# Moving loads, stores and vector work of a fused attention and dense kernel to other places and queues

## The chip, the cores and the metric

The kernel runs on one core of a Trainium2 chip. The metric is the device time in microseconds (us). An engine is one of PE (TensorE), DVE (VectorE), ACT (ScalarE), POOL (GpSimd) and SP (SyncE, which here only issues DMAs). The engines run their own instruction streams and meet at semaphores.

## The reference

The computation is cross attention followed by a 4-bit quantised dense layer, each with a layernorm ahead and a residual around it. All of it is float32.

```python
x = x + xattn(layernorm(x), ctx, ctx, pos, mask, Wq, Wk, Wv, Wo)   # x, ctx: (8, 256, 1024)
# xattn: 32 query heads, 8 key/value heads of 128; rope on q and k; masked softmax; @ Wo
x = x + (layernorm(x) @ W + bias)      # W = scales * (nibbles(qweight) - nibbles(qzeros))
```

## The kernel before

Every float32 product is made of three PE passes: each operand is split into a high part (a rounded copy, made by ACT) and a low part (the rest, a subtraction on DVE or POOL), and `products` multiplies high by high, high by low and low by high. So all operands pass through ACT and then through DVE or POOL before PE can use them.

The order of work is written out by hand, one stream per engine, in three stages:

1. **Keys and values.** 64 units of 24 matmuls each; the results go to scratch in DRAM. During the first key units DVE takes the statistics of the rows of x. `inverse_std` turns them into 1/std, PE transposes mean and 1/std in the value units `V_H0_N1` (L625 to L631), DVE copies them out (L1223 to L1227), and SP stores them and goes on with its queue (L358).
2. **Attention.** 16 groups (G) of 8 units (u8), one unit for each of 4 batches and 2 head pairs. In a unit PE computes scores of the next unit (12 short matmuls), half a query tile (12 matmuls), the weighted values of the unit two back (6 matmuls) and the other half of the query tile (12). The probabilities are transposed in a round trip: DVE writes `squares`, SP stores them (`store_squares`, L424), waits until they have landed, loads them back turned (`load_turned`, L434), ACT and POOL split them (L969, L1548), PE weighs. SP's stream is in order, so all its other loads and stores stand between these. Group 7 is the **switch**: the normalised activations `act_t` of the first half of the batches are replaced with those of the second, in eight pieces of 512 KB. Pieces 0 to 3 are for token half c=0 and 4 to 7 for c=1. Each piece is loaded into the low half (`load_next`, by SP), copied by ACT (`split_next`, L885) and subtracted by DVE (`rest_of_next`, L1175); PE waits for pairs of them (`next_lo`, L723, L730) in units 4 and 6. Also here DVE writes the masks of the second half (`set_mask`, L1256), and the rope tables are loaded.
3. **Output product and dense layer.** The product with Wo is done as seven half-size products M1 to M7 of 16 steps each (112 steps, counted s). A step needs a left tile (`xring`, from `left_scratch`) and one or two right blocks (`wraw`), loaded two steps ahead by `load_step(s)`, which waits until both operands of step s-2 are split. POOL adds the right blocks (`right_summed`, L1578), ACT splits, POOL and DVE take the low parts (`step_lo`), PE does 24 matmuls. Within the first ten steps the last attention results (pairs q = 62 and 63) are still combined (`combine`, POOL, five additions) and stored (`store_outputs`, `store_sums`, SP). From step 26 to 49 DVE and ACT unpack the dense weights between steps, and at each product's end (s = 17, 33, 49, ...) DVE adds eight PSUM banks into `rows` (`product_out`), which PE must await bank by bank before it starts the next product.

Of the kernel before, what the change touches and what calls it, by code (L numbers as in the profile page):

```python
# [9 lines left out]
F32 = mybir.dt.float32  # L10
# [59 lines left out]
def build(nc, x, ctx_t, x_tiles, x_pieces, pos, mask, wq, wk, wv, wo, qweight, qzeros, scales, bias, table, ident, out):  # L70
# [4 lines left out]
    with ExitStack() as stack:  # L75
# [208 lines left out]
        def _(sp):  # L284
# [97 lines left out]
            for u in range(16):  # L382
                g = u // 2
                if u % 2 == 0:
                    i = KVH + g + 2
# [62 lines left out]

            def load_next(i):

                sp.wait_ge(xc_stored[i % 4], 32)
                sp.wait_ge(q_done, 62 + 2 * (i // 4))
                sp.dma_start(next_rows(i, 1).bitcast(F32), xc_dram[i]).then_inc(next_in[i], 16)

            def attention(G, half, first=False, last=False, switch=False):
                g, nh = (0, 1) if switch else (G - half * 8 + 1, half)
                for u8 in range(UPG):
# [34 lines left out]
                    if switch:  # L492
                        if 2 <= u8 <= 5:
                            load_next(2 * u8 - 4)
                            load_next(2 * u8 - 3)
                        if u8 in (3, 5):
                            c = (u8 - 3) // 2
                            sp.wait_ge(q_rot, 62 + 2 * c)
                            sp.dma_start(rope[:, c, :, :], rope_dram[1, c]).then_inc(rope_in[c], 16)
# [43 lines left out]
            for s in range(4, STEPS):  # L543
                load_step(s)

                if s in (5, 7):
                    q = 62 + (s - 5) // 2
                    store_outputs(q, 31, q % 2)
                if s in (6, 9):
                    q = 62 + (s - 6) // 3  # L550
                    store_sums(q, 31, q % 2)
                if s < 20:
                    r = (s - 4 + 8) % 16
                    sp.dma_start(rows[:, r, :], x_rows[row_tile(r)]).then_inc(rows_in[r // 8], 16)

                if s == 20:
                    sp.dma_start(packed, qweight).then_inc(dense_in, 16)
                if s == 21:
                    sp.dma_start(scale_rows, scales.rearrange("r (a n) -> r a n", a=1).broadcast_to([KT, P // KT, E])
                                 ).then_inc(dense_in, 16)  # L560
                if s == 22:
                    sp.dma_start(zero_words[:, :],
                                 qzeros.rearrange("g (a w) -> g a w", a=1).broadcast_to([KT, P // KT, E // NIB])
                                 ).then_inc(dense_in, 16)
                if s == 23:
                    sp.dma_start(bias_rows[:, :], bias.rearrange("(a n) -> a n", a=1).broadcast_to([P, E])
                                 ).then_inc(bias_in, 16)
# [7 lines left out]
        def _(pe):  # L575
# [49 lines left out]
            for t in range(TT):  # L625
                value_unit(V_H0_N1 + t, items=C_WV1 if t == 0 else None)
                if t == 2:

# [196 lines left out]
        def _(act):  # L825
# [52 lines left out]
            def tile_hi(t):  # L878
                act.wait_ge(x_centred, 8 + t + 1)
                act.wait_ge(kv_done, V_H1_N0 + t + 1)  # L880
                act.activation(act_v[:, 0, :, t * P:(t + 1) * P], x_tile[t % 4], ACT.Copy).then_inc(x_hi, 1)

            def split_next(i):
                act.wait_ge(next_in[i], 16)
# [108 lines left out]
            def attention(G, first=False, last=False, switch=False):  # L993
                for u8 in range(UPG):
# [7 lines left out]
                    if switch and 3 <= u8 <= 6:  # L1002
                        split_next(2 * u8 - 6)
                        split_next(2 * u8 - 5)
                    if not (last and u8 >= 5):
                        i = (u8 + 3) % 4

                        scored = G * 16 + (2 * (u8 + 1 - i) + (0 if i < 2 else 4))
                        query_hi(TILES[i], G * UPG + (u8 + 3), None if first and u8 == 0 else scored)
                    if u8 < UPG - 1:  # L1010
                        nxt, nG = u8 + 1, G
# [18 lines left out]
                    if not (last and u8 == UPG - 1):  # L1030
                        scaled(nG, nxt)


# [26 lines left out]
            for s in range(2, STEPS):  # L1060
                step_hi(s)
                if s >= 28 and s % 3 == 1 and s < 52:
                    dense_hi((s - 28) // 3)
                if s == 92:
# [21 lines left out]
        def _(dve):  # L1086
# [134 lines left out]
            for t in range(TT):  # L1221
                value_lo(V_H0_N1 + t)
                if t == 3:  # L1223
                    dve.wait_ge(moments_turned, 1)
# [90 lines left out]
            def attention(G, half, first=False, switch=False, last=False):  # L1315
                for u8 in range(UPG):
# [33 lines left out]
                    if not (last and u8 == UPG - 1):  # L1350
                        inverse_sum(nG, nxt)
                    if switch and u8 >= 6:

                        for b1 in range(2):
                            set_mask(2 * (u8 - 6) + b1, 1)
                    if last and u8 in (6, 7):
# [64 lines left out]
            for s in range(2, STEPS):  # L1421
# [7 lines left out]
                step_lo(s)  # L1429
                if s == 26:  # L1430
                    dve.wait_ge(dense_in, 48)
                    for i in range(NIB):
                        dve.tensor_scalar(zeros_f.rearrange("p (w i) -> p w i", i=NIB)[:, :, i], zero_words[:, :],
                                          BITS * i, 2 ** BITS - 1, ALU.logical_shift_right,
                                          ALU.bitwise_and).then_inc(z_step, 1)
                if s == 27:
                    dve.wait_ge(z_step, NIB)
                if 27 <= s < 51:
                    if s % 3 == 0:
                        dense_full((s - 27) // 3)  # L1440
                    if s % 3 == 1:
                        dense_lo((s - 28) // 3)
                if 82 <= s < 90:
# [35 lines left out]
        def _(pool):  # L1479
# [134 lines left out]
            for s in range(2, STEPS):  # L1614
                step_lo(s)
                if s + 1 < STEPS:
                    right_summed(s + 1)
                if s in (3, 4, 6, 7):
                    q = 62 + (s - 3) // 3
                    combine(q, q % 2, s % 3)  # L1620
            pool.wait_ge(bias_in, 16)
# [38 lines left out]
```

## Time and profile before

| | |
|---|---|
| median of 3 runs | 2292.0 us (2291.43 to 2292.24) |
| the profiled execution, its device time | 2291.43 us |
| its span from first to last instruction | 2289.6 us |
| PE / DVE / ACT / POOL busy | 98% / 59% / 45% / 60% |
| DMA | 208 GB/s over the span |
| clock of PE granted over the span | 0.994 |

Span and device time differ by 1.8 us. PE's busy time leaves 55 us of the span. The trace has further stretches in which PE is busy but at the lower of its two clocks (granted 0.5 of full speed); a window's granted clock below 1.00 shows these.

### The profile page before, as it was taken

The numbers are of one execution on the slowest core, as the hardware profiler recorded it, in microseconds if no ns is written. First come the engines' busy times: TensorE is split into PE (matmuls) and PEld (weight loads), VectorE is DVE, ScalarE is ACT, GpSimd is POOL, SyncE is SP. The second block draws the span as 40 slices with busy tenths as digits, with TensorE's granted clock in tenths as the row PEclk, the third lists the DMA queues.
The fourth block names the chain that finished last, engine by engine and source line by source line (L and its number), as shares of the span: only waits on it lengthen the run. The fifth ranks groups of instructions, "written<-read, shape, count | busy, mean of one in ns | idle before, by whom it ended". The sixth has DMA issues, their size and how long they took to land.

```text
span 2289.6 us, 33278 instructions
## 1 busy us (share of the span) xinstructions
PE 2234.6 (98%) x10562; PEld 1865.2 (81%) x10562; DVE 1350.1 (59%) x2535; ACT 1040.8 (45%) x2264; POOL 1382.3 (60%) x981
## 2 busy tenths in 40 slices
PE   8999999999999998899999999899999999999999
PEld 6888887888888887688888888678887787878887
DVE  4772574777777777777777777423775324433432
ACT  3222123766776766667666676523332232321000
POOL 1320544788888986788888888665663353454210
PEclk9999999999999999999999999999999999999999
DMA  7766674678778878787878778587563454452111
GB/s 260 258 238 218 242 260 150 213 238 258 239 247 246 251 242 259 221 247 243 247 244 257 240 245 262 165 310 265 186 198 128 151 194 154 148 183 84 47 47 46
DMA packets 300779, 476.71 MB, mean 208 GB/s; under 512 B 23552, under 2 KB 195872, under 8 KB 300704
## 3 DMA queue, kind: packets, MB, share of 16 engines
q1 hardware_dynamic: 286624, 440.12, 59.8%
q10 hardware_dynamic: 13312, 33.56, 3.7%
q0 software_dynamic: 768, 2.10, 0.3%
q8 instruction: 39, 0.64, 0.1%
q14 instruction: 36, 0.29, 0.0%
HBM read 303.70 MB, written 171.98 MB: 208 GB/s over the span
## 4 chain that ended last, share of the span: by engine, by line
PE 84%; DVE 4%; DMA 4%; POOL 3%; SPq 2%; issue 1%; ACT 1%; ACTq 0%; POOLq 0%; DVEq 0%
PE ps L236 20%; PE ps L237 20%; PE ps L238 20%; PE ps L775 8%; PE ps L777 8%; PE ps L776 8%; DMA sq_scratch<-scores 3%; DVE rows L1392 1%; SPq L434 1%; PE ps L799 1%; DMA act_t<-xc_scratch 1%; POOL rope_tmp L1488 1%; POOL s_buf L1488 0%; DVE a_parts L1282 0%; DVE rows L1394 0%
## 5 line engine op out<-in xcount | busy, mean ns | idle before, releaser
L236 PE MATMUL ps<-act_t,wq_t 128*128 128x512 f32 x1280 | 502.2, 392 | 15.7 <-DVE act_t L1175 9.3
L237 PE MATMUL ps<-act_t,wq_t 128*128 128x512 f32 x1280 | 501.1, 392 | 0.0
L238 PE MATMUL ps<-act_t,wq_t 128*128 128x512 f32 x1280 | 499.4, 390 | 0.0
L1566 POOL TENSOR_TENSOR b_parts<-wraw,b_parts 128x512 fp32r<-128x512 f32 x112 | 196.5, 1754 | 277.2 <-ACT b_parts L991 277.2
L775 PE MATMUL ps<-b_parts,a_parts 128*128 128x512 f32 x896 | 352.3, 393 | 9.2 <-DVE rows L1392 4.9
L1282 DVE TENSOR_TENSOR a_parts<-xring,a_parts 128x1024 fp32r<-128x1024 f32 x112 | 147.5, 1317 | 344.4 <-ACT a_parts L986 344.4
L777 PE MATMUL ps<-b_parts,a_parts 128*128 128x512 f32 x896 | 349.5, 390 | 0.0
L776 PE MATMUL ps<-b_parts,a_parts 128*128 128x512 f32 x896 | 349.2, 390 | 0.0
L1548 POOL TENSOR_TENSOR q_t<-pt_raw,q_t 128x1024 fp32r<-128x1024 f32 x124 | 298.8, 2410 | 80.0 <-ACT q_t L969 78.3
L986 ACT ACTIVATE a_parts<-xring 128x1024 fp32r<-128x1024 f32 x112 | 118.8, 1060 | 421.7 <-PE ps L777 417.2
L236 PEld LDWEIGHTS ps<-act_t,wq_t 128*128 128x128 f32 x1280 | 241.8, 189 | 64.7 <-DVE act_t L1175 10.3
L1488 POOL TENSOR_TENSOR rope_tmp<-rope_tmp 128x512 f32<-128x512 f32 x144 | 193.5, 1344 | 155.1 <-DVE rope_tmp L1114 154.4
L238 PEld LDWEIGHTS ps<-act_t,wq_t 128*128 128x128 f32 x1280 | 241.3, 189 | 51.4
L237 PEld LDWEIGHTS ps<-act_t,wq_t 128*128 128x128 f32 x1280 | 241.8, 189 | 45.4
L951 ACT ACTIVATE probs<-scores,neg_max 128x256 f32<-128x256 f32 x512 | 253.9, 497 | 9.8 <-DVE neg_max L1271 9.6
L1112 DVE TENSOR_TENSOR rope_tmp<-ps,rope 128x512 f32<-128x512 f32 x144 | 99.4, 690 | 211.2 <-PE ps L238 190.3
L961 ACT ACTIVATE probs<-probs,inv_sum 128x256 f32<-128x256 f32 x512 | 216.9, 495 | 1.8 <-DVE inv_sum L1278 1.8
L943 ACT ACTIVATE q_t<-rope_tmp 128x512 fp32r<-128x512 f32 x128 | 81.0, 633 | 294.4 <-POOL rope_tmp L1488 294.4
L775 PEld LDWEIGHTS ps<-b_parts,a_parts 128*128 128x128 f32 x896 | 168.5, 188 | 55.8 <-DVE rows L1392 8.7
L1537 POOL TENSOR_TENSOR q_t<-rope_tmp,q_t 128x512 fp32r<-128x512 f32 x128 | 196.1, 1532 | 20.3 <-ACT q_t L943 20.2
L777 PEld LDWEIGHTS ps<-b_parts,a_parts 128*128 128x128 f32 x896 | 168.5, 188 | 35.3
L776 PEld LDWEIGHTS ps<-b_parts,a_parts 128*128 128x128 f32 x896 | 168.6, 188 | 33.8
(129 smaller groups left out, 4329.1 us busy)
## 6 DMA issues: line engine op xcount, KB each, us to landing
sq_scratch<-scores SPq DMA_DIRECT2D x124, 512.0 KB, 4.7
pt_raw<-sq_scratch SPq DMA_DIRECT2D x496, 128.0 KB, 3.1
xring<-left_scratch SPq DMA_DIRECT2D x112, 512.0 KB, 3.9
left_scratch<-s_buf SPq DMA_DIRECT2D x64, 640.0 KB, 4.8
wraw<-in_L_xattn_Wq SPq DMA_DIRECT2D x64, 512.0 KB, 4.8
wraw<-in_L_xattn_Wo SPq DMA_DIRECT2D x64, 512.0 KB, 4.8
v_scratch<-kv_t ACTq DMA_DIRECT2D x32, 512.0 KB, 3.2
k_scratch<-kv_t ACTq DMA_DIRECT2D x32, 512.0 KB, 4.9
```

What stands on the lines that cost most here:

```text
L236: eng.matmul(dst, lh, rh, start=(k == first), stop=False)
L237: eng.matmul(dst, lh, rl, start=False, stop=False)
L238: mm = eng.matmul(dst, ll, rh, start=False, stop=(k == last))
L775: pe.matmul(dst, lh, rh, start=(begins and not onto), stop=False, skip_group_check=True)
L776: pe.matmul(dst, lh, rl, start=False, stop=False, skip_group_check=True)
L777: mm = pe.matmul(dst, ll, rh, start=False, stop=ends, skip_group_check=True)
L951: e = act.activation(probs[:, par, j, qt, :], score_v[:, par, j, qt * S:(qt + 1) * S], ACT.Exp, bias=neg_max[:, par, j, qt:qt + 1], scale= ...
L961: e = act.activation(probs[:, par, j, qt, :], probs[:, par, j, qt, :], ACT.Copy, scale=inv_sum[:, par, j, qt:qt + 1])
L1488: pool.tensor_tensor(tmp[:, 0, :], tmp[:, 0, :], tmp[:, 1, :], ALU.add).then_inc(done, 1)
L1537: pool.tensor_tensor(q_parts[:, c, j, 1, :], rope_tmp[:, 0, :], q_parts[:, c, j, 0, :].bitcast(F32), ALU.subtract).then_inc(q_lo, 1)
L1548: pool.tensor_tensor(lo, pt_raw[:, u8 % 2, :], hi.bitcast(F32), ALU.subtract).then_inc(pt_lo, 1)
L1566: pool.tensor_tensor(b_parts[:, s % 2, 1, :], wraw[s % 2][:, 0:NW], b_parts[:, s % 2, 0, :].bitcast(F32), ALU.subtract).then_inc(right_lo, 1)
```

## The change

The change has five parts.

- **Activation pieces at the switch.** `load_next` leaves SP's stream. ACT issues the pieces, four at once, after `query_hi` in units 2 and 4. ACT's `split_next` calls are spread: one before `query_hi` and one at the end of a unit, from the end of unit 2 to unit 6.
- **Masks at the switch.** One `set_mask` at the end of each of units 3 to 6 instead of two at the end of units 6 and 7.
- **Moments.** The two PE transposes and DVE's copy stand one value unit earlier.
- **Last results.** POOL combines q = 62 wholly after step 3 and q = 63 after step 5. SP stores both the outputs and the sums of each ahead of `load_step(5)` and `load_step(7)`.
- **Dense weights.** The four loads are issued together at s = 20 (before, at 20 to 23), and unpacking runs from s = 23 to 46 (before, 26 to 49).

```diff
-            def load_next(i):
-                sp.wait_ge(xc_stored[i % 4], 32)
-                sp.wait_ge(q_done, 62 + 2 * (i // 4))
-                sp.dma_start(next_rows(i, 1).bitcast(F32), xc_dram[i]).then_inc(next_in[i], 16)
...
-                        if 2 <= u8 <= 5:
-                            load_next(2 * u8 - 4)
-                            load_next(2 * u8 - 3)
...
             for s in range(4, STEPS):
-                load_step(s)
-
                 if s in (5, 7):
                     q = 62 + (s - 5) // 2
                     store_outputs(q, 31, q % 2)
-                if s in (6, 9):
-                    q = 62 + (s - 6) // 3
                     store_sums(q, 31, q % 2)
+                load_step(s)
...
-                if t == 2:
+                if t == 1:
                     pe.wait_ge(ln_ready, 1)
...
+            def load_next(c):
+                for b in range(4):
+                    act.wait_ge(xc_stored[b], 32)
+                act.wait_ge(q_done, 62 + 2 * c)
+                for i in range(4 * c, 4 * c + 4):
+                    act.dma_start(next_rows(i, 1).bitcast(F32), xc_dram[i]).then_inc(next_in[i], 16)
...
                     if switch and 3 <= u8 <= 6:
-                        split_next(2 * u8 - 6)
                         split_next(2 * u8 - 5)
...
+                    if switch and u8 in (2, 4):
+                        load_next(u8 // 2 - 1)
...
+                    if switch and 2 <= u8 <= 5:
+                        split_next(2 * u8 - 4)
...
-                    if switch and u8 >= 6:
-                        for b1 in range(2):
-                            set_mask(2 * (u8 - 6) + b1, 1)
+                    if switch and u8 >= 3 and u8 < 7:
+                        set_mask(u8 - 3, 1)
...
-                if 27 <= s < 51:
+                if 24 <= s < 48:
                     if s % 3 == 0:
-                        dense_full((s - 27) // 3)
+                        dense_full((s - 24) // 3)
...
-                if s in (3, 4, 6, 7):
-                    q = 62 + (s - 3) // 3
-                    combine(q, q % 2, s % 3)
+                if s in (3, 5):
+                    q = 62 + (s - 3) // 2
+                    for part in range(2):
+                        combine(q, q % 2, part)
```

ACT's stream in the switch, from `query_hi` of unit 2 on, before:

```order
L943 ACTIVATE q_t<-rope_tmp 128x512
L951 ACTIVATE probs,row_sum<-scores,neg_max 128x256 x4
L969 ACTIVATE q_t<-pt_raw 128x1024
L961 ACTIVATE probs<-probs,inv_sum 128x256 x4
L843 ACTIVATE wq_t<-wraw 128x8x128
L885 ACTIVATE act_t<-act_t 128x2x512 x2
L943 ACTIVATE q_t<-rope_tmp 128x512
```

and the same place of the change, where `act_t<-xc_scratch` are the pieces' loads and `act_t<-act_t` their copies:

```order
L936 ACTIVATE q_t<-rope_tmp 128x512
L874 DMA act_t<-xc_scratch 128x2x512 x4
L944 ACTIVATE probs,row_sum<-scores,neg_max 128x256 x4
L962 ACTIVATE q_t<-pt_raw 128x1024
L954 ACTIVATE probs<-probs,inv_sum 128x256 x4
L878 ACTIVATE act_t<-act_t 128x2x512
L828 ACTIVATE wq_t<-wraw 128x8x128
L878 ACTIVATE act_t<-act_t 128x2x512
L936 ACTIVATE q_t<-rope_tmp 128x512
```

Four loads now stand ahead of the exponentials of unit 2, and one copy has moved ahead of the head split (`wq_t<-wraw`).

SP's queue from the loads of step 5 to those of step 7, before (`left_scratch<-o_buf` are outputs, `left_scratch<-s_buf` are sums):

```order
L515 DMA xring<-left_scratch 128x2x512
L521 DMA wraw<-in_L_xattn_Wo 128x512
L522 DMA wraw<-in_L_xattn_Wo 128x512
L441 DMA left_scratch<-o_buf 128x256
L442 DMA left_scratch<-o_buf 128x256
L554 DMA rows<-in_x 128x1024
L515 DMA xring<-left_scratch 128x2x512
L521 DMA wraw<-in_L_xattn_Wo 128x512
L522 DMA wraw<-in_L_xattn_Wo 128x512
L447 DMA left_scratch<-s_buf 128x5x256
L554 DMA rows<-in_x 128x1024
L515 DMA xring<-left_scratch 128x2x512
```

and in the change, from after the rows of step 4 to the first load of step 6:

```order
L441 DMA left_scratch<-o_buf 128x256
L442 DMA left_scratch<-o_buf 128x256
L447 DMA left_scratch<-s_buf 128x5x256
L506 DMA xring<-left_scratch 128x2x512
L512 DMA wraw<-in_L_xattn_Wo 128x512
L513 DMA wraw<-in_L_xattn_Wo 128x512
L543 DMA rows<-in_x 128x1024
L506 DMA xring<-left_scratch 128x2x512
```

The loads of step 5 now stand behind the sums of q = 62, which wait for POOL.

DVE's stream at the end of product M4, s = 48 and 49, before:

```order
L1282 TENSOR_TENSOR a_parts<-xring,a_parts 128x1024 x2
L1399 TENSOR_SCALAR dense<-dense 128x1024
L1402 TENSOR_TENSOR dense<-dense 128x1024
L1404 TENSOR_TENSOR dense<-dense 128x1024
L1392 TENSOR_TENSOR rows<-ps,rows 128x512 x16
L1282 TENSOR_TENSOR a_parts<-xring,a_parts 128x1024
```

and in the change:

```order
L1403 TENSOR_TENSOR w_parts<-dense,w_parts 128x1024
L1278 TENSOR_TENSOR a_parts<-xring,a_parts 128x1024 x2
L1387 TENSOR_TENSOR rows<-ps,rows 128x512 x16
L1278 TENSOR_TENSOR a_parts<-xring,a_parts 128x1024 x16
```

No unpacking stands between the last left tile and the 16 additions any more.

## Rows read from the trace of the kernel before

**Rows 1.** PE's waits: who, for whom, us in total, times, longest.

```profile
PE ps L236 <- DVE act_t L1175: 9.3, 2, 8.5
...
PE ps L236 <- DVE wq_t L1103: 0.6, 2, 0.4
```

**Rows 2.** Windows: stretch, length, each engine's busy us, granted clock, DMA share, GB/s.

```profile
840.00:860.00 20.00, 20.00 (x105) 17.19 (x104) 15.17 (x34) 15.70 (x38) 17.44 (x13) 1.00 0.80 256
880.00:900.00 20.00, 13.47 (x54) 10.67 (x53) 13.88 (x26) 11.50 (x23) 12.37 (x10) 0.83 0.94 298
...
1720.00:1740.00 20.00, 17.32 (x67) 12.77 (x66) 15.72 (x19) 5.69 (x7) 5.44 (x4) 0.91 0.35 119
1740.00:1760.00 20.00, 19.36 (x83) 15.04 (x83) 7.92 (x9) 4.83 (x7) 5.47 (x3) 1.00 0.40 130
...
1820.00:1840.00 20.00, 18.94 (x79) 14.02 (x78) 13.45 (x20) 5.56 (x7) 8.30 (x6) 1.00 0.58 193
```

**Rows 3.** Timeline of DVE in the switch: start, us, line, operation, idle before.

```profile
875.72 0.69 DVE L1112 TENSOR_TENSOR rope_tmp<-ps,rope 128x512 f32<-128x512 f32 x1 [1.84 <-PE ps L238]
887.53 1.23 DVE L1175 TENSOR_TENSOR act_t<-act_t 128x1024 fp32r<-128x1024 f32 x1 [0.66 <-ACT act_t L885]
937.52 4.07 DVE L1256 TENSOR_SCALAR scores<-mask 128x512 f32<-128x512 uint8 x2
957.25 0.69 DVE L1112 TENSOR_TENSOR rope_tmp<-ps,rope 128x512 f32<-128x512 f32 x1 [1.94 <-PE ps L238]
```

**Rows 4.** Timeline of PE in the switch, matmuls after long waits.

```profile
891.07 0.77 PE L236 MATMUL ps<-act_t,wq_t 128*128 128x512 f32 x1 [5.69 <-issue]
925.99 0.79 PE L236 MATMUL ps<-act_t,wq_t 128*128 128x512 f32 x1 [8.50 <-DVE act_t L1175]
```

**Rows 5.** Chain of waits in the switch: start, us, what.

```profile
872.61 4.80 DMA sq_scratch<-scores
...
905.38 9.34 DMA sq_scratch<-scores
```

**Rows 6.** Timeline of SP and ACT around unit 2 of the switch.

```profile
879.53 1.19 SPq L453 DMA_DIRECT2D act_t<-xc_scratch  x2
870.96 0.63 ACT L943 ACTIVATE q_t<-rope_tmp 128x512 fp32r<-128x512 f32 x1 [2.31 <-POOL rope_tmp L1488]
875.45 1.06 ACT L969 ACTIVATE q_t<-pt_raw 128x1024 fp32r<-128x1024 f32 x1 [1.77 <-DMA pt_raw<-sq_scratch]
```

**Rows 7.** Timeline of PE and DVE around the transposed moments.

```profile
159.33 0.27 PE L630 MATMUL ps<-identity,mean_var 128*16 128x128 f32 x1
157.61 0.17 DVE L1160 TENSOR_TENSOR inv_std<-ln_tmp 128x16 f32<-128x16 f32 x1
```

**Rows 8.** Timeline of SP in steps 5 and 7 of the output product.

```profile
1482.46 0.38 SPq L515 DMA_DIRECT2D xring<-left_scratch  x1
1492.95 0.39 SPq L447 DMA_DIRECT2D left_scratch<-s_buf  x1
```

**Rows 9.** Timeline of POOL and ACT in the same steps.

```profile
1484.83 0.74 POOL L1557 TENSOR_TENSOR s_buf<-o_buf 128x256 f32<-128x256 f32 x1
1492.81 1.29 POOL L1566 TENSOR_TENSOR b_parts<-wraw,b_parts 128x512 fp32r<-128x512 f32 x1
1501.91 2.23 POOL L1578 TENSOR_TENSOR wraw<-wraw 128x512 f32<-128x512 f32 x1 [3.21 <-DMA wraw<-in_L_xattn_Wo]
1489.79 1.06 ACT L986 ACTIVATE a_parts<-xring 128x1024 fp32r<-128x1024 f32 x1 [3.86 <-PE ps L777]
...
1530.11 1.07 ACT L986 ACTIVATE a_parts<-xring 128x1024 fp32r<-128x1024 f32 x1 [4.00 <-PE ps L777]
```

**Rows 10.** Timeline of DVE and PE at the end of product M4.

```profile
1728.19 1.78 DVE L1399 TENSOR_SCALAR dense<-dense 128x1024 int32<-128x1024 int32 x1
1732.41 9.65 DVE L1392 TENSOR_TENSOR rows<-ps,rows 128x512 f32<-128x512 f32 x16
1733.84 0.47 PE L775 MATMUL ps<-b_parts,a_parts 128*128 128x512 f32 x1 [2.48 <-DVE rows L1392]
```

More of the change, by code:

```diff
@@ L557, in _ @@
                     sp.dma_start(packed, qweight).then_inc(dense_in, 16)
-                if s == 21:
                     sp.dma_start(scale_rows, scales.rearrange("r (a n) -> r a n", a=1).broadcast_to([KT, P // KT, E])
                                  ).then_inc(dense_in, 16)
-                if s == 22:
                     sp.dma_start(zero_words[:, :],
@@ L564, in _ @@
                                  ).then_inc(dense_in, 16)
-                if s == 23:
                     sp.dma_start(bias_rows[:, :], bias.rearrange("(a n) -> a n", a=1).broadcast_to([P, E])
@@ L1061, in _ @@
                 step_hi(s)
-                if s >= 28 and s % 3 == 1 and s < 52:
-                    dense_hi((s - 28) // 3)
+                if s >= 25 and s % 3 == 1 and s < 49:
+                    dense_hi((s - 25) // 3)
                 if s == 92:
@@ L1222, in _ @@
                 value_lo(V_H0_N1 + t)
-                if t == 3:
+                if t == 2:
                     dve.wait_ge(moments_turned, 1)
@@ L1429, in _ @@
                 step_lo(s)
-                if s == 26:
+                if s == 23:
                     dve.wait_ge(dense_in, 48)
@@ L1435, in _ @@
                                           ALU.bitwise_and).then_inc(z_step, 1)
-                if s == 27:
+                if s == 24:
                     dve.wait_ge(z_step, NIB)
-                if 27 <= s < 51:
+                if 24 <= s < 48:
                     if s % 3 == 0:
-                        dense_full((s - 27) // 3)
+                        dense_full((s - 24) // 3)
                     if s % 3 == 1:
-                        dense_lo((s - 28) // 3)
+                        dense_lo((s - 25) // 3)
                 if 82 <= s < 90:
```

## The prediction

> **What bounds the kernel now.** I read the page first: PE is busy for 98% of the span, so a change pays only where PE waits or where it delays PE. Next came PE's waits. The longest single one, 8.5 us, is for DVE L1175, the low parts of the pieces at the switch [rows 1]. The windows then show where time is lost. Around the switch PE has 13.47 us of work in 20 and a granted clock of 0.83, while 20 us at 840 are full. At 1720, the end of M4, it has 17.32 us at 0.91, and 19.36 in the next 20 [rows 2]. A clock of 0.91 over 20 us is some 3.6 us at the lower level (1.2 GHz instead of 2.4), which costs half of that, 1.8 us. It follows an idle of 2.48 us [rows 10]. In the switch, idles of 5.69 and 8.50 us precede or meet the lower clock [rows 4]. I take it that each idle as long as these costs another 1.7 to 1.8 us.
>
> What the switch costs comes from DVE's rotations, one per unit. From 875.72 to 957.25 there are seven intervals, 81.53 us [rows 3]. A full unit is 8.26 us: 30 long matmuls, one per 0.227, make 6.8, and twelve short ones at 0.12 make 1.4 (PE works without a gap there, the window at 840 [rows 2]). Seven are 57.8. So the switch costs 23.7 us.
>
> **Part 1, the switch.** Now the pieces are issued at 879.53, behind SP's wait for the squares stored at 872.61 [rows 5, 6]. The data is free earlier: `query_hi` of unit 2 (870.96) already implies that PE is done with token half c=0. After the change four issues of 0.59 us (half of 1.19 for two) begin there, so the exponentials start 1.8 us later, at 873.4, and end at 875.4. ACT waited 1.77 us for the turned probabilities until 875.45 anyway, so this costs nothing. I follow the chain with the durations of the trace:
>
> - ACT rescales by 878.3, copies piece 0 (1.06), splits the head and copies piece 1 by 881.3.
> - DVE, done with the row maxima at 880.9, subtracts pieces 0 and 1 (1.23 each [rows 3]) by 883.3 and the head by 884.6. PE wants them at 885.4, after the scores of unit 4. The wait of 5.69 us goes.
> - Pieces 2 and 3: ACT copies the latter by 889.9. DVE rotates (2.1), transposes (1.25) and subtracts both by 891.8. The mask that now ends unit 3 falls beside POOL's 2.4 us subtraction. The masks of 937.52 took 4.07 us for two beside POOL's work [rows 3], so it may add up to 2: 893.8. PE wants them at 889.5. New wait: 2.3 to 4.3.
> - Pieces 4 and 5 are issued at 890 and copied by 899.6, subtracted by 903.0, wanted at 904.1: no wait. Piece 7 is subtracted at 910.4, wanted at 908.3: a wait of 2.1, where 8.50 stood.
>
> That is 4.4 to 6.4 us. But the DMA engines must carry it. Normal units use them at 0.80 with 256 GB/s, the switch at 0.94 with 298 [rows 2], so about 317 GB/s is full. The eight pieces and two rope tables are 5.2 MB, 14 to 16 us of full DMA; in the 42 us from 871 to 913 some 8.5 are free. The lack of 6 to 8 us is not on top of the waits, since they give it time, but the larger counts: 8. With one more stretch at the lower clock (1.7 to 1.8) the switch costs 10 instead of 23.7: **-13.7**. Bounds: the chain alone with no clock loss costs 5 (-18.7); a store of squares as slow as the one of 905.38, 9.34 us instead of 4.80 [rows 5], in each of the units costs 17 (-6.7). The masks no longer delay the first unit of group 8; this is inside.
>
> The Trainium skill (DMA: Bandwidth & Descriptors, section on queues, rings and completion order) says that each DMA engine takes turns between the queues that have work. By that rule SP's squares get only a part of the engines while ACT's 2 MB are in the queue, and the sum would lean to the upper bound, -6.7. The trace does not show the two queues together in this stage.
>
> **Part 2, the moments.** The transposes run at 159.33 [rows 7], right behind the third value unit. That unit is 24 matmuls at 0.227, so the second ends at 153.9, and the transposes now stand there. They need 1/std, which DVE finishes at 157.78; nothing of that chain waits for PE. At their old place that was 1.5 us in time. PE will idle 3.9 us. All work up to the attention hangs on PE's units, and from there to 384 PE has only two waits, 0.6 us in all, for DVE L1103 [rows 1], so nothing gives it back. An idle of 3.9 should bring the lower clock once: **+5.6** (3.9 + 1.7). Bounds: 3.3 if the later small idles close up, 7.3 with two such stretches. The earlier copy of the moments helps transfers that PE did not wait for: nothing.
>
> **Part 3, the last results.** In M1 PE needs 24 matmuls at 0.227, 5.44 us, for a step. Before, POOL's five additions stood in two portions between step operands, and the loads of step 5 were issued at 1482.46 [rows 8]. Now:
>
> - POOL's additions for q = 62 run from 1484.83 [rows 9] in one piece, 0.70 each apart from one beside DVE work, to 1489.35. The low part of step 4 follows at 1490.6, and PE waits 0.9 (it ended step 3 at 1489.75, for which ACT waited at 1489.79 [rows 9]).
> - SP waits for the sums, stores them and issues the loads of step 5 at 1489.9, 7.4 us later than before. How long they take: after the sums of 1492.95 [rows 8], 512 KB of rows and the loads of step 7, POOL got its right blocks at 1501.91 [rows 9], 8.95 us. Without the rows (1.6 us at 317 GB/s) it is 7.3: landing at 1496.7. Then POOL adds (1.3, or 2.23 beside DVE work [rows 9]), ACT splits (0.63 for this size [rows 6]), POOL subtracts (1.29 [rows 9]): 1500.4. PE is ready at 1496.1: a wait of 4.3.
> - Step 6: loads land at 1501.7, POOL adds to 1503.0, then combines q = 63 to 1507.5, then the low part, 1508.8. PE is ready at 1505.9: 2.9.
> - Step 7: its loads stand behind these sums too: 1507.6 + 7.3 = 1514.9, operands at 1518.2. PE is ready at 1514.3: 3.9.
> - From step 8 on the loads keep up.
>
> PE starts step 7 at 1518.2 and with four steps of 5.44 ends step 10 at 1540.0. Before, it did at 1530.1, where ACT's row of 1530.11 waits for it [rows 9]. That is +9.9. Stretches at the lower clock inside the waits cost nothing, since the loads decide; the last one costs 1.7. **+11.6**. Bounds: loads landing 2 us sooner throughout give +5.7; landing 1 us later for both and every wait with its clock loss +16.
>
> **Part 4, the dense weights.** At the end of M4 DVE unpacked from 1728.19 and began the 16 additions at 1732.41, so PE waited 2.48 us and then four short times, 3.3 in all, and lost 1.8 to the clock [rows 2, 10]. Without the 4.2 us of unpacking the additions start at 1728.3, and this end looks as that of the next product does, which also has 16 operations: 20 - 18.94 = 1.06 us and a clock of 1.00 [rows 2]. That is -2.2 - 1.7 = **-3.9**. Three steps earlier the unpacking meets no other product's end in a new place. The four loads together put 1.6 MB before the loads of s = 21, when a step moves 1 MB and its loads lead by two steps: nothing, at most +1.
>
> **Sum.** -13.7 + 5.6 + 11.6 - 3.9 = -0.4 us against 2291.43 of the profiled execution. That execution was the fastest of three, 0.6 under the median of 2292.0, so the forecast is 2291.5: no change. This kernel's measurement can tell about 0.2%, 4.6 us, from none.
>
> **Rivals.**
>
> - *The queue is less full than I think* (faster). The rows that I time the M1 loads by had stores and rows before and after them; with DMAs idle from 1485 to 1489 the loads may land 2 us sooner each, and part 3 costs 5.7. For it: nothing is in the queue then. Against: the store of the sums goes out with them. -0.4 - 5.9 = -6.3: 2285.7. With the switch at its best as well it is 2281.
> - *ACT's queue starves SP's round trip* (slower). SP waits for each store of squares before it loads them. From the point where store, turned load and the issues between take over 8.26 us, SP is late every unit and PE waits at `weigh`. Both happened at 905.38, at 9.34 us. For it: 2 MB at once beside SP's 1.5 to 2.4 MB a unit. Against: the same 2 MB went through SP's own queue, where they stood in front of the squares. Part 1 gives 6.7 instead of 13.7: +6.6, 2298.6. The skill's rule above is this rival in a sentence.
>
> **Chances.** The forecast 0.40, the first rival 0.33, the second 0.27. All lower bounds together give -18.7 + 3.3 + 5.7 - 3.9 = -13.6, all upper ones -6.7 + 7.3 + 16 - 2.9 = +13.7. Three quarters of each way hold the time 8 times in 10: 2281 to 2301. Faster by over 0.2%: 0.33; within 0.2%: 0.40; slower: 0.27. The forecast's own range is 2287 to 2296.
>
> **What would show it.** Right: an idle of PE of about 3.9 us at 154; PE waits after steps 3, 4, 5 and 6 of M1 of 0.9, 4.3, 2.9 and 3.9, released by POOL L1561 (the low parts); the end of M4 with 1.06 us of idle and clock 1.00; no idle over 4.5 us in the switch, and 68 us instead of 81.5 for the seven intervals. Wrong: PE waits in M1 under 5 us in sum, or stores of squares above 8 us throughout the switch, or an idle of over 5 us there for `next_lo`.

## The result

The changed kernel takes 2305.6 us (median of 5 runs, 2300.57 to 2308.26), the kernel before beside it 2292.0. The ratio is 1.0057, 95% interval 1.0044 to 1.0069: slower by 13.6 us by the medians, where 2291.5 and no change had been forecast. The profiled execution took 2304.1 us, its span is 2302.3 (before 2289.6).

Three heads of PE's waits in the changed kernel (who, for whom, us in total, times, longest) differ from the kernel before: the wait for POOL's `b_parts` was 1.6 us in two times there, the one for `inv_std` did not exist, and the one for `act_t` was 9.3 us with a longest of 8.5 [rows 1].

```profile
PE ps L760 <- POOL b_parts L1561: 13.8, 4, 4.8
...
PE ps L236 <- DVE act_t L1171: 4.4, 2, 2.7
...
PE ps L615 <- DVE inv_std L1156: 3.8, 1, 3.8
```

The windows of the changed kernel, beside [rows 2] (stretch, length, busy us of PE, PEld, DVE, ACT, POOL, granted clock, DMA share, GB/s):

```profile
880.00:900.00 20.00, 15.34 (x77) 12.72 (x76) 12.47 (x22) 12.38 (x29) 12.87 (x10) 0.99 0.88 276
900.00:920.00 20.00, 17.34 (x73) 14.10 (x73) 19.25 (x36) 14.33 (x32) 15.15 (x11) 0.84 1.03 314
...
1480.00:1500.00 20.00, 15.33 (x67) 12.08 (x65) 3.75 (x4) 4.61 (x6) 11.97 (x10) 1.00 0.70 238
1500.00:1520.00 20.00, 14.74 (x53) 11.72 (x54) 4.09 (x3) 3.26 (x4) 12.90 (x11) 0.85 0.66 224
1580.00:1600.00 20.00, 16.13 (x71) 13.13 (x70) 4.61 (x4) 5.22 (x7) 8.89 (x6) 0.98 0.74 221
1720.00:1740.00 20.00, 20.00 (x90) 16.57 (x89) 15.41 (x9) 7.39 (x9) 12.32 (x8) 1.00 0.57 196
1740.00:1760.00 20.00, 18.93 (x79) 13.99 (x78) 13.15 (x19) 4.74 (x6) 5.76 (x4) 1.00 0.37 120
```

The switch is fuller than it was (880 to 900). The first product (1480 to 1520) is emptier: the kernel before has 20.00 and 19.16 us of PE work in these two windows. The window at 1580 is new: the kernel before is full there. The end of M4, now at 1745, has the 1.07 us of idle and the clock of 1.00 that were expected.

PE's timeline in the changed kernel (start, us, line, operation, idle before and its releaser) puts a place to each:

```profile
158.85 0.39 PE L615 MATMUL ps<-identity,mean_var 128*16 128x128 f32 x1 [3.79 <-DVE inv_std L1156]
...
890.44 0.47 PE L236 MATMUL ps<-q_t,kv_t 128*128 128x512 f32 x1 [2.70 <-POOL q_t L1543]
898.19 0.47 PE L236 MATMUL ps<-act_t,wq_t 128*128 128x512 f32 x1 [1.96 <-issue]
906.79 0.79 PE L236 MATMUL ps<-act_t,wq_t 128*128 128x512 f32 x1 [2.66 <-DVE act_t L1171]
926.69 0.50 PE L236 MATMUL ps<-act_t,wq_t 128*128 128x512 f32 x1 [1.71 <-DVE act_t L1171]
...
1490.10 0.47 PE L760 MATMUL ps<-b_parts,a_parts 128*128 128x512 f32 x1 [0.47 <-POOL b_parts L1561]
1500.49 0.77 PE L760 MATMUL ps<-b_parts,a_parts 128*128 128x512 f32 x1 [4.68 <-POOL b_parts L1561]
1517.95 0.77 PE L760 MATMUL ps<-b_parts,a_parts 128*128 128x512 f32 x1 [4.78 <-POOL b_parts L1561]
1599.58 0.77 PE L760 MATMUL ps<-b_parts,a_parts 128*128 128x512 f32 x1 [3.87 <-POOL b_parts L1561]
```

A matmul of 0.77 us instead of 0.47 is one at the lower clock: over 1500 to 1503, behind the wait of 4.68 us, the granted clock is 0.55.

DVE's timeline, the two rotations that bound the seven intervals of [rows 3]:

```profile
884.10 0.68 DVE L1108 TENSOR_TENSOR rope_tmp<-ps,rope 128x512 f32<-128x512 f32 x1
...
954.52 0.69 DVE L1108 TENSOR_TENSOR rope_tmp<-ps,rope 128x512 f32<-128x512 f32 x1 [1.57 <-PE ps L238]
```

Seven intervals now take 70.42 us, not 81.53. ACT's first operation of a step (`step_hi`) gives the same scale for the products. The one that began at 1530.11 [rows 9] begins here:

```profile
1541.34 1.06 ACT L979 ACTIVATE a_parts<-xring 128x1024 fp32r<-128x1024 f32 x1 [3.86 <-PE ps L762]
```

The lag behind the kernel before, taken from the same instruction in both traces, splits the 12.7 us of span:

| stretch | forecast | in the changed kernel's trace |
|---|---|---|
| moments (62 to 238) | +5.6 | +6.3 |
| 238 to 876 | 0 | +1.8 |
| the switch's seven intervals | -13.7 | -11.1 |
| 957 to 1429, given back | 0 | +2.4 |
| last results (to 1541) | +11.6 | +11.5 |
| dense loads (1590 to 1625) | 0 | +5.6 |
| end of M4 | -3.9 | -4.2 |

The rows add up to 12.3 us; most of the rest is 0.3 us by which PE's very first wait is longer (9.23 us instead of 8.91). Of the 6.3 us of the moments, 0.7 arise by 85, ahead of the transposes; across them the lag grows by 5.6.

### The profile page after: what moved, and what is told of

Same layout as the page of the kernel before. It is cut to its first block, busy times and chain, and to the rows that moved or that the text cites. A ratio compares the mean times of both kernels' runs of the same rounds, so it can differ in the third digit from the quotient of the medians.

```text
span 2302.3 us, 33274 instructions
## 1 busy us (share of the span) xinstructions
PE 2239.5 (97%) x10562; PEld 1867.5 (81%) x10562; DVE 1353.1 (59%) x2535; ACT 1041.1 (45%) x2264; POOL 1386.0 (60%) x981
## 4 chain that ended last, share of the span: by engine, by line
PE 76%; DVE 7%; DMA 5%; POOL 5%; issue 2%; SPq 2%; ACT 2%; ACTq 0%; POOLq 0%; DVEq 0%
PE ps L236 18%; PE ps L238 17%; PE ps L237 17%; PE ps L760 8%; PE ps L762 8%; PE ps L761 8%; DMA sq_scratch<-scores 4%; DVE rows L1387 1%; POOL s_buf L1483 1%; SPq L434 1%; DMA wraw<-in_L_xattn_Wo 1%; POOL rope_tmp L1483 1%; ACT wq_t L828 1%; POOL q_t L1543 1%; PE ps L784 1%
## 5 line engine op out<-in xcount | busy, mean ns | idle before, releaser
L936 ACT ACTIVATE q_t<-rope_tmp 128x512 fp32r<-128x512 f32 x128 | 81.1, 633 | 283.1 <-POOL rope_tmp L1483 283.1
```

## The experiments

All times are medians in us of 5 to 23 runs; "before" is the kernel before, run beside it on the same chip.

| run | this | before | ratio, 95% interval |
|---|---|---|---|
| switch_only | 2286.44 | 2294.34 | 0.9964, 0.9951 to 0.9978 |
| moments_only | 2300.08 | 2294.34 | 1.0027, 1.0018 to 1.0037 |
| last_only | 2307.52 | 2294.34 | 1.0061, 1.0048 to 1.0075 |
| dense_only | 2296.28 | 2294.34 | 1.0007, 0.9998 to 1.0016 |
| dense_loads_only | 2299.68 | 2292.99 | 1.0032, 1.0020 to 1.0045 |
| dense_compute_only | 2288.59 | 2292.99 | 0.9982, 0.9973 to 0.9991 |
| plain_sources | 2295.48 | 2294.03 | 1.0004, 0.9995 to 1.0013 |
| combine_only | 2300.06 | 2292.99 | 1.0032, 1.0020 to 1.0045 |
| first_result_ahead | 2300.28 | 2294.48 | 1.0029, 1.0018 to 1.0040 |
| first_result_behind | 2296.21 | 2294.48 | 1.0006, 0.9998 to 1.0015 |
| masks_only | 2291.75 | 2294.34 | 0.9989, 0.9980 to 0.9997 |
| act_loads_in_pairs | 2284.92 | 2294.34 | 0.9960, 0.9947 to 0.9973 |
| sp_loads_in_fours | 2286.21 | 2294.34 | 0.9965, 0.9953 to 0.9978 |
| sp_loads_in_pairs | 2290.75 | 2294.34 | 0.9986, 0.9977 to 0.9994 |
| switch_and_dense_compute | 2281.02 | 2292.99 | 0.9951, 0.9938 to 0.9965 |
| act_pairs_and_dense_compute | 2281.44 | 2294.48 | 0.9948, 0.9932 to 0.9963 |

**One part at a time.** The four parts were put into the kernel before, each alone, with the parts' lines as in the diff above.

> The kernel before with part 1 alone (the eight loads of the next batch's pieces from ACT in two lots of four, the splits and the masks one per unit). Theory A, read from the two traces: part 1 gains what the lags show, 10.5 us until PE 946 and about 8.5 us by 1429, and the rest of the loss is the other parts': 2283.5 us (2281 to 2286), four PE waits of 2 to 3 us each in the units around 890 to 926 and two short falls of the clock. Theory B: part 1 by itself is worth the 13.7 us that the prediction gave it, and only starting it 6.6 us later behind the moments' wait has spoilt its meeting with the other transfers: 2278.3 us. Theory C: it gains nothing by itself: 2292.

> The kernel before with part 2 alone (the two transposes of the moments one tile earlier on PE, the copy one tile earlier on DVE). Theory A: one PE wait of 3.8 us for inv_std before the transpose and a fall of the clock to 0.5 of 3.4 us behind it, nothing given back later: 2297.6 us (2297 to 2298.5). Rival: the later stages have slack that takes part of it back (the waits of the key and value units for their weights, or the waits of 1.7 and 1.1 us at 390 to 400): 2294 us or less.

> The kernel before with part 3 alone (POOL combines the last two results each in one go, SP stores outputs and sums ahead of load_step of steps 5 and 7). Theory A: load_step(5) is issued 7 us later than in the kernel before and load_step(7) likewise, PE waits 4.7 us before step 5 and 4.8 us before step 7 and the clock falls twice: 2304.5 us (2303 to 2306). Rival B: part of the 12.5 us that the changed kernel lost in this stage was brought by the switch's end coming at another moment: 2300 us or less.

> The kernel before with part 4 alone (the four loads of the dense weights together in step 20, the dequantizing three steps earlier). Theory A: the four loads stand in the queue ahead of step 21's load, which lands in about 12 us instead of 5, PE waits about 3.9 us before step 22 or 23 and the clock falls once, +5.5 us, and the end of the fourth product gives 4.2 us back: 2293.3 us (2292 to 2294.5). Rival B, the prediction's: the four loads are hidden and only the gain at the end of the fourth product stays: 2288.1 us, with no PE wait over 1 us between 1560 and 1620.

Against the kernel before they bring -7.9, +5.7, +13.2 and +1.9 us, in sum +12.9; all together bring +13.6. The parts add, so the loss is not in their meeting. For the switch theory A held in size: part 1 is worth about 8 us by itself and not 13.7. Its four waits were not "2 to 3 us each" but 1.64, 2.15, 4.66 and 1.68. In moments_only the wait of 3.79 us stands again, at 159.77, and the rival (slack further on takes it back) falls. In last_only PE waits 0.97, 4.67 and 2.98 us before steps 4, 5 and 7, so the 4.7 of theory A came and its 4.8 did not. dense_only has a wait of 4.20 us at 1593.84 in a kernel whose first product is untouched, so that wait is the dense part's own.

**The dense weights: loads or unpacking.** In one kernel only the loads are together:

```diff
                 if s == 20:
                     sp.dma_start(packed, qweight).then_inc(dense_in, 16)
-                if s == 21:
                     sp.dma_start(scale_rows, ...
-                if s == 22:
                     sp.dma_start(zero_words[:, :], ...
-                if s == 23:
                     sp.dma_start(bias_rows[:, :], ...
```

and in the other only DVE's and ACT's unpacking stands three steps earlier.

> The kernel before with its four dense loads all in step 20; the dequantizing stays where it was. Theory A (the loads standing ahead of step 21's and 22's cost the time): step 22's transfer takes about 12 us, one PE wait of about 3.9 us near 1580, a fall of the clock, and no gain at the end of the fourth product: +5.5 us on the kernel before. Rival (the wait comes from DVE or ACT doing the dequantizing earlier, not from the loads): +0, no wait near 1580.

> The kernel before with the dequantizing three steps earlier and the four loads one per step as before. Theory A: no PE wait near 1580 and the gain at the end of the fourth product stays (no wait of 2.5 us, no fall of the clock there): -4.0 us on the kernel before (-4.5 to -3.3). Rival (earlier dequantizing costs something, or its data come too late for step 23 when loaded in steps 20 to 22): -1 us or worse, with DVE or PE waits near step 23.

+6.7 and -4.4 us: both theories A. The chain of waits of dense_loads_only (start, us, what) names the transfer:

```profile
1575.04 11.51 DMA wraw<-in_L_xattn_Wo
1586.62 2.19 POOL wraw L1575
1588.83 0.64 ACT b_parts L988
1589.54 1.28 POOL b_parts L1563
1590.82 0.14 issue
1590.95 0.69 PE ps L772
```

PE waited 3.61 us at its end (at 1590.95), so a transfer of 7.9 us would have been hidden by the two steps by which the loads lead. Its windows show why the load is late:

```profile
1572.00:1574.00 2.00, 2.00 (x10) 1.69 (x9) 1.23 (x1) 0.65 (x2) 1.28 (x1) 1.00 1.05 413
...
1576.00:1578.00 2.00, 2.00 (x11) 1.65 (x10) 0.41 (x1) 1.50 (x2) 0.00 (x0) 1.00 1.03 157
...
1580.00:1582.00 2.00, 2.00 (x11) 1.65 (x10) 0.00 (x0) 0.00 (x0) 0.00 (x0) 1.00 1.12 179
1582.00:1584.00 2.00, 2.00 (x10) 1.67 (x9) 0.00 (x0) 0.00 (x0) 0.00 (x0) 1.00 0.98 365
```

The DMA engines are busy in all four, but from 1576 to 1582 they move 156 to 179 GB/s, where it is 413 before and 365 after. Three of the four loads read rows of DRAM that are repeated over many partitions: the scales (8 rows, each 16 times, 512 KB), the bias (one row, 128 times, 512 KB) and the zero points (64 KB). plain_sources reads scales and bias from ordinary tiles of `x` of the same size, so its dense weights and bias are wrong ones:

```diff
-sp.dma_start(scale_rows, scales.rearrange(...).broadcast_to([KT, P // KT, E]))
+sp.dma_start(scale_rows, x_rows[row_tile(0)])
-sp.dma_start(bias_rows[:, :], bias.rearrange(...).broadcast_to([P, E]))
+sp.dma_start(bias_rows[:, :], x_rows[row_tile(1)])
```

> The same four loads together in step 20 as in dense_loads_only, but the scales and the bias (512 KB each, rows of DRAM repeated over many partitions) are read from two ordinary tiles of x of the same size instead; so the dense weights and the bias are wrong ones, all else is the same. Theory A (the repeated rows make the transfer slow: 157 to 179 GB/s at full DMA share for 8 us, where ordinary loads reach 413): the load of step 22 lands within 8 us, PE waits under 1 us near 1590, +1 us or less on the kernel before. Rival B (1.6 MB more in the queue is the cost, whatever the source): PE waits 3.6 us again and the kernel is 5 to 7 us slower than before.

Its windows over the same place:

```profile
1574.00:1578.00 4.00, 4.00 (x19) 3.34 (x18) 1.23 (x1) 0.85 (x2) 3.06 (x2) 1.00 1.02 392
1578.00:1582.00 4.00, 4.00 (x19) 3.30 (x19) 1.23 (x1) 1.58 (x2) 1.64 (x1) 1.00 0.97 359
```

PE has no wait there, and the kernel's 1.5 us over the one before can't be told from none (0.9995 to 1.0013). The bytes are the same as in dense_loads_only. So the sources with repeated rows are the cost, not the 1.6 MB. The run swaps both at once and does not say which of them is slow. The kernel before, where they go one per step, has a hint: its bias load is issued at 1583.56 right behind the 1 MB of step 23 and lands 5.6 us later, and the window over it is a fast one:

```profile
1585.00:1588.00 3.00, 3.00 (x15) 2.49 (x14) 1.57 (x1) 1.21 (x2) 2.25 (x2) 1.00 1.04 416
```

Its slow stretch (1578 to 1582, shown further down) stands behind the load of the scales. So a repeated row is not slow in every load; a run with the scales alone swapped would settle it, and there is none.

**The last results: POOL or SP.** combine_only has POOL's additions as changed, but SP stores behind the loads:

```diff
                 load_step(s)
                 if s in (5, 7):
                     q = 62 + (s - 5) // 2
                     store_outputs(q, 31, q % 2)
-                if s in (6, 9):
-                    q = 62 + (s - 6) // 3
                     store_sums(q, 31, q % 2)
```

> The kernel before with POOL's combining of the last two results in one go each (after steps 3 and 5, as in the changed kernel), but with SP's stores of outputs and sums behind load_step(5) and load_step(7), not ahead. Theory A (what costs is that SP holds load_step until POOL has combined): load_step(5) goes out near 1482.5 again, PE waits under 1 us before step 5; load_step(6) and (8) now stand behind the stores, but these wait little; total 0 to +3 us on the kernel before. Rival B (what costs is POOL's five sums in a row ahead of its part of the step): PE waits 4 us and more again, +9 to +13 us.

+7.1 us, between the theories: neither is the whole. The loads of step 5 go out at 1483.45 as A said, and PE waits 1.10 us before step 4 and not before step 5. But POOL's timeline has the second result's five additions between the two operations of step 6:

```profile
1499.21 2.23 POOL L1576 TENSOR_TENSOR wraw<-wraw 128x512 f32<-128x512 f32 x1 [4.03 <-DMA wraw<-in_L_xattn_Wo]
1501.41 0.74 POOL L1555 TENSOR_TENSOR s_buf<-o_buf 128x256 f32<-128x256 f32 x1
...
1504.17 1.75 POOL L1560 TENSOR_TENSOR s_buf<-o_buf 128x256 f32<-128x256 f32 x1
1505.88 1.26 POOL L1564 TENSOR_TENSOR b_parts<-wraw,b_parts 128x512 fp32r<-128x512 f32 x1
```

and PE waits 4.30 us for that low part:

```profile
1507.28 0.47 PE L773 MATMUL ps<-b_parts,a_parts 128*128 128x512 f32 x1 [4.30 <-POOL b_parts L1564]
```

Two kernels then change the first result alone, POOL in one go after step 3, SP's stores ahead of load_step(5) or behind it; the second result stays as before.

> The kernel before with only the first of the two last results as in the changed kernel: POOL combines it in one go after step 3, SP stores its outputs and sums ahead of load_step(5); the second result stays as it was. Theory A (SP's held load is what costs here): load_step(5) goes out 6 to 7 us later, PE waits 4.7 us before step 5 and the clock falls once, +6 us on the kernel before. Rival B (the wait before step 5 is POOL's doing): the same +6 us here and in first_result_behind.

> The same, but with SP's stores of the first result behind load_step(5). Theory A: load_step(5) goes out near 1483 again, no PE wait over 1.2 us before steps 4 to 6, and, since the second result's combining is in two halves again, none of 4.3 us before step 7: within +1.5 us of the kernel before, 4 to 6 us below first_result_ahead. Rival B: +6 us as in first_result_ahead.

+5.8 and +1.7 us (the latter's interval holds zero). In first_result_ahead, SP holds the loads until 1492.31; at 1483.45 they go in first_result_behind. SP's timeline of first_result_ahead:

```profile
1491.83 0.38 SPq L447 DMA_DIRECT2D left_scratch<-s_buf  x1
1492.31 0.47 SPq L515 DMA_DIRECT2D xring<-left_scratch  x1
```

and its PE:

```profile
1493.09 0.47 PE L776 MATMUL ps<-b_parts,a_parts 128*128 128x512 f32 x1 [1.98 <-POOL b_parts L1567]
1503.42 0.47 PE L776 MATMUL ps<-b_parts,a_parts 128*128 128x512 f32 x1 [2.99 <-POOL b_parts L1567]
```

Theory A's direction holds, though its wait of 4.7 us before step 5 was 2.99, with 1.98 a step earlier. By differences of medians, each good to some 3 us: the first result's additions in one go cost 1.7, the second's 7.1 - 1.7 = 5.4, and SP's held loads 4.1 for one result, 13.2 - 7.1 = 6.1 for both. SP's stores ahead with POOL's additions in halves was not tried: the second half of the second result stands behind step 7, whose loads would wait for it.

**The switch: where its gain comes from.** masks_only moves only the masks. The three others have splits and masks as changed and differ in who issues the eight loads, and in what lots.

```diff
 act_loads_in_pairs (ACT)
+                    if switch and 2 <= u8 <= 5:
+                        load_next(u8 - 2)
 sp_loads_in_fours (SP, load_next as before)
-                        if 2 <= u8 <= 5:
-                            load_next(2 * u8 - 4)
-                            load_next(2 * u8 - 3)
+                        if u8 in (2, 4):
+                            for i in range(4):
+                                load_next(2 * u8 - 4 + i)
```

> The kernel before with DVE's four masks one per unit in units 3 to 6 and nothing else of part 1. Theory A (the gain of part 1 is that the pieces come earlier, so PE's wait of 8.5 us for DVE's act_t near 926 goes): the masks alone give 0 to -1.5 us, and the wait of 7 to 8.5 us near 926 stays. Rival (the gain is the masks, two of which take 4.07 us each beside POOL near 937 and hold DVE): -6 us or more.

> Part 1 as in the changed kernel, but ACT issues the eight loads in pairs in units 2 to 5 instead of four in unit 2 and four in unit 4. Theory A (what part 1 still pays is that four loads of 512 KB at once stand before the store of squares, which then takes 10.4 us instead of 5 to 6 near 881): the store near 881 lands in 6 to 8 us, the PE waits of 885 and 893 shrink, and the gain is 2 to 4 us larger than part 1's -7.9: -10 to -12 on the kernel before. Rival B (the pieces of a pair land too late for the split at the end of the same unit, so ACT stalls and with it the softmax): smaller gain, -5 us or less.

> Part 1 with the masks and the splits as changed, but the loads stay on SP, four at the end of its unit 2 and four at the end of its unit 4. Theory A (what matters is when the bytes move, not which engine issues them): within 2 us of part 1's -7.9. Rival B (ACT's issuing matters: SP's own loads and stores queue behind four loads on SP's queue, or the wait for q_done holds SP, or the ACT issue of 0.6 us each is saved): 3 us or more away from -7.9, to either side; if the queue is shared by issue order, the next load_turned after the four lands later and the result is worse, -4 us or less of a gain.

> The kernel before with the masks and the splits as changed, and the loads where they were (SP, two at the end of its units 2 to 5). Theory A (splits can't be earlier than the loads; a split at the end of ACT's unit now waits for a piece issued in the same unit and holds ACT's next softmax): no gain, 0 to +6 us on the kernel before. Rival B (spreading the splits and masks is where the gain comes from): -5 us or more.

-2.6, -9.4, -8.1 and -3.6 us. In lots of four, which engine issues makes no difference that can be told (-7.9 in switch_only, -8.1 from SP). On ACT, lots of four against pairs neither (-7.9 and -9.4). In pairs ACT is 5.8 us ahead of SP, since SP reaches its place 10 us later. So what parts the runs into two groups is when the lot with the last two pieces is issued. At 915.7 (masks_only) and 918.3 (sp_loads_in_pairs) PE's late wait for `act_t` is 6.72 and 6.87 us; at 908.3 (act_loads_in_pairs) it is 2.14, at 903.3 (sp_loads_in_fours) 2.28, and at 898.6 (switch_only) 1.68. Inside the early group the order doesn't follow the time of issue.

The mechanisms of two expectations did not come out. In act_loads_in_pairs the store of squares of 875.43 took 9.0 us and not 6 to 8, and PE waited 4.32 us behind it (at 885.42), more than the 1.64 of switch_only. The result of sp_loads_in_pairs lies between its theories, and the masks alone (-2.6) gave more than the 1.5 us expected at most.

PE's timeline of sp_loads_in_pairs:

```profile
926.76 0.79 PE L236 MATMUL ps<-act_t,wq_t 128*128 128x512 f32 x1 [6.87 <-DVE act_t L1176]
```

PE's of switch_only:

```profile
884.10 0.47 PE L236 MATMUL ps<-q_t,kv_t 128*128 128x512 f32 x1 [1.64 <-POOL q_t L1549]
892.01 0.47 PE L236 MATMUL ps<-act_t,wq_t 128*128 128x512 f32 x1 [2.15 <-issue]
901.18 0.80 PE L236 MATMUL ps<-act_t,wq_t 128*128 128x512 f32 x1 [4.66 <-DVE act_t L1177]
921.11 0.51 PE L236 MATMUL ps<-act_t,wq_t 128*128 128x512 f32 x1 [1.68 <-DVE act_t L1177]
```

**A version that beats both.** Part 1 with the earlier unpacking, its four loads one per step as before; moments and last results as before.

> The kernel before with part 1 and with the dequantizing three steps earlier, without the bunched dense loads, the moments' move and the last results' move. If the parts add: -7.9 (part 1 alone) and -4.0 (expected of the dequantizing) = -11.9 us on the kernel before, about 2282.5 us on a chip where the kernel before takes 2294.3. Rival (they don't add, since what is gained at the switch is lost again in waits of the units behind it): -8 us or less of a gain.

> The kernel before with part 1, its eight loads in pairs on ACT, and with the dequantizing three steps earlier with its loads one per step. If the parts add: -9.4 and -4.4 = -13.8 us on the kernel before (-11 to -15). Rival (the pairs are no better than the fours, the 1.5 us between them was scatter): -12 us, as the version with the fours.

2281.02 and 2281.44 us, -12.0 and -13.0 against the kernel before. The parts add here too (-7.9 - 4.4 = -12.3), and pairs are no better than fours by any difference that can be told.

## Why the prediction was wrong

The sum came to -0.4 us and the measurement to +13.6. Three terms held, two failed. (Two slips of arithmetic changed nothing: 5.2 MB at 317 GB/s are 16.5 us and not 14 to 16, and three quarters of +13.7 reach to 2302, not 2301.)

- **Moments: right in mechanism and size.** An idle of 3.9 and one fall of the clock, +5.6; measured an idle of 3.79 us, and +5.7 alone.
- **Last results: the sum was right, its shares were not.** +11.6 forecast, +11.5 in the trace, +13.2 alone. The loads of step 5 went out at 1489.30 (forecast 1489.9) and POOL had its blocks at 1496.09 (1496.7). The waits before steps 4 to 7 were 0.47, 4.68, none and 4.78, where 0.9, 4.3, 2.9 and 3.9 stood: step 6 did not wait, since its loads went out right behind those of step 5, at 1491.98, and step 5 itself ran long at the lower clock. That the sum came out is in part luck: PE waited 9.9 us and not 12.0, and there were two falls of the clock (3.4 us, from the granted clocks of 0.85 and 0.98 over 1500 to 1540) where one of 1.7 was counted. Both mechanisms of the working, SP's held loads and POOL's additions in one piece, were measured apart (6.1 and 7.1 us).
- **End of M4: right.** -3.9 forecast, -4.2 in the trace, -4.4 alone.
- **The four dense loads: the step that failed.** They were given "nothing, at most +1", because 1.6 MB beside the 1 MB of a step were set against a lead of two steps, with no transfer time worked out for them. They cost 5.6 in the trace and 6.7 alone: the load behind them took 11.51 us, where 7.9 would have been hidden. Bytes alone do not make that, as plain_sources shows; the sources with repeated rows do, at 156 to 179 GB/s. (The 317 GB/s that the working of part 1 holds for full was too low, with 413 in a window, but that errs the other way.) A window of the kernel before would have shown the slow stretch. Behind the load of the scales, which it issued at 1572.67:

```profile
1578.00:1582.00 4.00, 4.00 (x19) 3.34 (x18) 1.23 (x1) 1.58 (x2) 2.32 (x2) 1.00 0.97 189
```

- **The switch: the size of the term failed.** -13.7 forecast, -7.9 alone. In the changed kernel's trace the seven intervals brought -11.1, and 2.4 were given back behind them: -8.7. Two waits were forecast as none: 2.70 us at 890.44 for the turned probabilities, and 1.96 at 898.19. The working took the duration of the store of squares from its old rows (4.80 [rows 5]). The chain of the changed kernel has:

```profile
881.28 10.42 DMA sq_scratch<-scores
```

It shares the engines with the four pieces. The DMA queues from 884 to 889 in the changed kernel, while the store and the pieces are both in flight (packets, MB, share of 16 engines):

```profile
q10 hardware_dynamic: 660, 1.29, 81.1%
q1 hardware_dynamic: 577, 0.35, 26.4%
```

SP's queue (q1) gets nearly as many packets through as ACT's (q10), but they are a third as large, and ACT's queue has three quarters of the time. The Trainium skill (DMA: Bandwidth & Descriptors, section on queues, rings and completion order) says that a DMA engine takes turns between queues with work; by the number of packets the trace agrees, by time and bytes the turns are far from equal. But this isn't the reason of the missing gain by itself: the same page, in its section "Issuing engines are not separate DMA queues", says that issuing from several engines saves only issue time, and the pair of switch_only and sp_loads_in_fours (-7.9 and -8.1 us) agrees with that. The store took 7.8 us with SP's fours, and PE waited 5.86 at 891.43, where it waited 2.15 in switch_only. The rival "ACT's queue starves SP's round trip" was thus right that a store would double, once, and its price for part 1 (6.7) is nearer to the measured 7.9 than the forecast's 13.7. It was wrong about its point: SP was not late in every unit (the next four stores took 3.7, 4.0, 7.2 and 6.6 us).
- The other waits of the switch, 2.66 and 1.71 us, are the forecast 2.3 to 4.3 and 2.1. That leaves 2.4 us given back after 957. The lag shows 1.1 of it by 982 and 1.4 by 990, with waits of 0.17 to 0.24 us for POOL's `q_t`. What it is that runs tighter there was not settled; nor was the +1.8 between 238 and 876, where one wait of 0.97 us at 552.75 is new and is in no other trace of the study.

Of the rivals, "the queue is less full than I think" fell for the first product: POOL had its blocks 7.3 us after the store of the sums at 1488.81, as forecast.

## What to carry to other kernels

Before transfers are bunched, take their time from a window of the trace in which each kind is in the queue; a count of bytes against the lead of the loads hid the term that failed most (nothing forecast, 6.7 us measured). A store or wait put ahead of a load in an issuing engine's stream delays every load behind it (here from 1483.45 to 1492.31), and work in one piece between the two operations of a step costs what exceeds the slack of that step (here waits of 1.10 and 4.30 us). When changes are bundled, price them one by one: here two pieces were worth -12 us together (switch, earlier unpacking) and three cost 25.6 (5.7, 13.2, 6.7).

## What the runs showed of the hardware

- With the loads of scales and bias in the queue, whose source rows are repeated over partitions, the engines moved 156 to 179 GB/s at a DMA share of 1.00 to 1.12 (dense_loads_only); with ordinary rows in their place 359 to 392 at 0.97 to 1.02 (plain_sources). Not every such load is slow: that of the bias stands in a window of 416 in the kernel before.
- Two queues that are both busy got nearly equal numbers of packets (660 and 577 in 5 us), and 81.1% and 26.4% of the engines' time, with the packets of one three times as large (changed kernel, 884 to 889).
- POOL's additions of 128x256 take 0.72 to 0.74 us, but one that begins while DVE subtracts takes 1.72 to 1.78. In combine_only the one of 1504.17 does so; DVE's subtraction began at 1504.11. In the changed kernel all five from 1502.52 on take 0.73 or 0.74, with DVE idle. The second result's five additions thus vary by 1 us with where DVE stands.
